# A hand-ordered attention stack: POOL's norm of attention a step later, squares and context for the unit four ahead

## What is computed

```python
x  = layernorm(x + mha(x, x, mask, bias))            # stage 0, LN of attention
x2 = layernorm(x + mha(x, ctx))                      # stage 1, LN of attention
x  = layernorm(x2 + gelu(x2 @ w1 + b1) @ w2 + b2)    # stage 1, feed-forward and its LN
q, c = rmsnorm(x, g_q), rmsnorm(ctx, g_c)            # stage 2, norm of the inputs
out = rmsnorm(x + mha(q, c) , g_out)                 # stage 2, norm of attention
```

## Time and profile before

| | |
|---|---|
| median of 3 runs | 727.37 us (725.52 to 729.23) |
| profiled execution, its own time | 729.24 us |
| its span | 727.4 us, mean granted TensorE clock 0.94 |
| busy: PE, DVE, ScalarE, POOL | 600.9, 443.3, 430.1, 339.7 us |

### The profile page before, as it was taken

One profiled execution on the slowest core, in us unless ns is written; L12 is line 12 of the kernel. 1 busy time (PEld: TensorE's weight loads), 2 busy tenths in 40 slices (PEclk: granted clock), 3 DMA queues, 4 the chain that ended last, 5 costly groups with the idle time before them and its releaser, 6 DMA issues.

```text
span 727.4 us, 17247 instructions
## 1 busy us (share of the span) xinstructions
PE 600.9 (83%) x6804; PEld 311.8 (43%) x6804; DVE 443.3 (61%) x884; ACT 430.1 (59%) x658; POOL 339.7 (47%) x642
## 2 busy tenths in 40 slices
PE   3699988886799999989896959688696968998984
PEld 1346555544344444544443425243344434443442
DVE  5324444435878887877673747566375758887831
ACT  2034444442267778786684756658485858886683
POOL 5234666654443544446246282635345365463212
PEclk9999999998889999999998989989798989999997
DMA  6723333433606625335260322406051515435000
GB/s 192 181 62 97 99 94 95 106 110 61 146 30 125 133 57 106 97 73 109 38 123 27 89 37 69 79 24 125 24 112 46 109 46 110 125 63 118 2 9 16
DMA packets 85382, 61.18 MB, mean 84 GB/s; under 512 B 5474, under 2 KB 84882, under 8 KB 85266
## 3 DMA queue, kind: packets, MB, share of 16 engines
q1 hardware_dynamic: 85176, 59.97, 36.2%
q10 hardware_dynamic: 126, 0.10, 0.0%
HBM read 33.25 MB, written 26.22 MB: 82 GB/s over the span
## 4 chain that ended last, share of the span: by engine, by line
PE 38%; POOL 19%; DMA 16%; DVE 9%; issue 8%; ACT 6%; SPq 4%; POOLq 0%; DVEq 0%; ACTq 0%
DMA kst<-k_parts 10%; PE pv L555 9%; PE dps L537 6%; DVE negmax L810 5%; DMA k_parts<-ks 4%; PE aps L505 4%; PE aps L608 3%; ACT probs L679 3%; PE dps L643 2%; POOL attn_z L967 2%; PE aps L587 2%; PE dps L626 2%; PE dps L530 2%; POOL ks L930 2%; PE dps L524 1%
## 5 line engine op out<-in xcount | busy, mean ns | idle before, releaser
L679 ACT ACTIVATE probs<-aps 128x1024 f32<-128x1024 f32 x288 | 293.7, 1024 | 206.0 <-PE aps L505 140.7
L810 DVE TENSOR_REDUCE negmax<-dps 128x1 f32<-128x512 f32 x512 | 324.1, 682 | 113.9 <-PE dps L537 112.7
L555 PE MATMUL pv<-probs,vp 128*32 128x256 f32 (+1 forms) x3072 | 162.8, 340 | 1.9 <-ACT raw L732 1.1
L537 PE MATMUL dps<-kst,qst 61*128 61x512 bf16 x512 | 130.0, 403 | 34.8 <-DMA kst<-k_parts 19.8
L505 PE MATMUL aps<-qst,kst 64*128 64x256 bf16 x1024 | 115.0, 278 | 5.6 <-ACT probs L679 5.4
L555 PEld LDWEIGHTS pv<-probs,vp 128*32 128x32 f32 x3072 | 71.7, 113 | 56.7 <-issue 23.5
L537 PEld LDWEIGHTS dps<-kst,qst 61*128 61x128 bf16 x512 | 32.2, 93 | 132.6 <-DVE negmax L810 74.3
L926 POOL TENSOR_TENSOR kr<-kf,ks 128x512 f32<-128x512 f32 (+1 forms) x24 | 23.9, 996 | 113.1 <-ACT ks L696 69.8
L837 DVE COPY mT<-dps 24x256 bf16<-24x256 bf16 x48 | 13.2, 274 | 91.3 <-PE dps L637 91.2
L505 PEld LDWEIGHTS aps<-qst,kst 64*128 64x128 bf16 x1024 | 48.9, 97 | 43.3 <-ACT probs L679 14.4
L806 DVE TENSOR_REDUCE negmax<-dps 128x4 f32<-128x512 f32 x64 | 42.9, 687 | 28.9 <-PE dps L530 28.9
(11 more groups left out here) (126 smaller groups left out, 841.4 us busy)
## 6 DMA issues: line engine op xcount, KB each, us to landing
kst<-k_parts SPq DMA_DIRECT2D x32, 384.0 KB, 6.8
qst<-q_parts SPq DMA_DIRECT2D x48, 192.0 KB, 3.8
k_parts<-ks SPq DMA_DIRECT2D x16, 384.0 KB, 2.6
q_parts<-qs SPq DMA_DIRECT2D x24, 192.0 KB, 1.9
cin<-in_ctx_dram SPq DMA_DIRECT2D x16, 256.0 KB, 5.3
k_parts<-ks SPq DMA_DIRECT2D x16, 256.0 KB, 3.0
q_parts<-qs SPq DMA_DIRECT2D x24, 128.0 KB, 1.9
k_parts<-ks SPq DMA_DIRECT2D x24, 128.0 KB, 3.0
```

The costliest lines, as they stand in the source:

```text
L537: mm = nc.tensor.matmul(dst, q[rows_in(g, 0, ROW_M), l, tile * P:(tile + 1) * P], k[rows_in(g, 0, ROW_M), l, :], start=True, stop=True)
L555: mm = nc.tensor.matmul(pv[32 * j:32 * j + 32, dst:dst + n], vp[u.parity][:, c, 4 * quad + j, :], probs[:, quad, src:src + n], start=(quad ...
L679: nc.scalar.activation(probs[:, quad, part * 1024:(part + 1) * 1024], src, ACT.Exp, scale=SCALE).then_inc(act_emptied, 1)
L810: ins = nc.vector.tensor_reduce(negmax[:, tile, at:at + 1], src, AX.X, ALU.max, negate=True)
```

## The change

Three things move, and no operation is added or removed.

1. POOL's `finish_attention` for a unit runs one step later: in step i for unit i-2 (`old`) in place of unit i-1. Within the step it stands right behind the split of K, ahead of `split_maxima(nxt, 0)`, where `main` is of stage 1 or 2, and right behind `split_maxima(nxt, 0)` where `main` is of stage 0. The last unit's is done after the loop.
2. ScalarE's squares are those of unit i+4 (`far`) in place of unit i+3, at the same places of the strings. POOL's `norm_inputs` still serves unit i+3.
3. SP loads the context of unit i+4 in place of i+3, behind the load of M1's rows in place of ahead of it, and stores a result one step later.

```diff
--- before.py
+++ after.py
@@ -86,10 +86,12 @@
 
 
 
+
     def __init__(self, i):
         self.i = i
         self.main, self.nxt, self.n, self.ahead = unit(i), unit(i + 1), unit(i + 2), unit(i + 3)
-        self.before = unit(i - 1)
+        self.far = unit(i + 4)
+        self.before, self.old = unit(i - 1), unit(i - 2)
         self.ffn, self.ffn_old = (u if u is not None and u.stage == 1 else None for u in (unit(i - 2), unit(i - 3)))
         self.items = [item for item in self.all_items() if item[1] is not None]
 
@@ -128,8 +130,8 @@
             elif name == "raw":
                 yield "raw", self.before, None
             elif name in SQUARES_OF:
-                ahead = self.ahead
-                yield "squares", ahead if ahead is not None and ahead.stage == 2 else None, SQUARES_OF[name]
+                far = self.far
+                yield "squares", far if far is not None and far.stage == 2 else None, SQUARES_OF[name]
             elif name == "B3":
                 known = self.before is not None
                 yield "values", self.before, (3, ALL if known and self.before.stage == 0 else (2, 3))
@@ -419,6 +421,11 @@
                     sp.dma_start(k[rows_in(g, 0, ROW_X), :, col:col + nk],
                                  kd_rows[:, LOCAL * g:LOCAL * g + LOCAL, 0:nk]).then_inc(stacks_loaded, 16)
 
+            def store_out(u):
+                sp.wait_ge(attn_norm.scaled, u.index + 1)
+                sp.dma_start(out[u.batch].rearrange("(t p) d -> p t d", p=P), attn_norm.zg[:, :, :]
+                             ).then_inc(out_stored, 16)
+
             def load_maxima(u, half):
                 mine = slice(LOCAL // 2 * half, LOCAL // 2 * half + LOCAL // 2)
                 sp.wait_ge(dve_emptied, DVE_AT[f"M{half}", u.index] + 1)
@@ -436,10 +443,10 @@
                 if s.i == 2:
                     sp.wait_ge(mask_made, 1)
                     sp.dma_start(kmd, kmask[:, :]).then_inc(mask_stored, 16)
-                if s.ahead is not None and s.ahead.stage > 0:
-                    load_context(s.ahead)
                 if s.main is not None:
                     load_maxima(s.main, 1)
+                if s.far is not None and s.far.stage > 0:
+                    load_context(s.far)
                 if s.n is not None:
                     if s.n.index == 2 * B:
                         sp.wait_ge(mask_stored, 16)
@@ -454,10 +461,9 @@
                     load_maxima(s.nxt, 0)
                 if s.n is not None and not early:
                     load_stacks(s.n)
-                if s.before is not None and s.before.stage == 2:
-                    sp.wait_ge(attn_norm.scaled, s.before.index + 1)
-                    sp.dma_start(out[s.before.batch].rearrange("(t p) d -> p t d", p=P), attn_norm.zg[:, :, :]
-                                 ).then_inc(out_stored, 16)
+                if s.old is not None and s.old.stage == 2:
+                    store_out(s.old)
+            store_out(unit(UNITS - 1))
             sp.wait_ge(out_stored, 16 * B)
 
         @block.tensor
@@ -1004,14 +1010,19 @@
                 if s.n is not None:
                     split(s.n, qf, qr, qs, LQ, "Q", q_steps)
                     split(s.n, kf, kr, ks, KEYS[s.n.stage], "K", k_steps)
+
+                late = s.main is not None and s.main.stage == 0
+                if s.old is not None and not late:
+                    finish_attention(s.old)
                 if s.nxt is not None:
                     split_maxima(s.nxt, 0)
+                if s.old is not None and late:
+                    finish_attention(s.old)
                 if s.ahead is not None and s.ahead.stage == 2:
                     norm_inputs(s.ahead)
                 if s.ffn_old is not None:
                     layer_norm(ffn_norm, s.ffn_old, in_cross(s.ffn_old), 2, xs[:, s.ffn_old.batch, :, :], x_ready)
-                if s.before is not None:
-                    finish_attention(s.before)
+            finish_attention(unit(UNITS - 1))
 
 
 # ---- launch: one core; constants of the shapes, and the weights laid out
```

## The result

The changed kernel takes 753.11 us (median of 4 runs, 749.47 to 757.41), against 728.3 of the kernel before in the same runs: a ratio of 1.0341, with a 95% interval of 1.0265 to 1.0417. It is 3.4% slower, where I had forecast 2.7% faster. The profiled execution took 749.47 us, its span is 747.7, the mean granted clock 0.926.

What follows compares the result with a forecast made beforehand. No engine bounds throughout; PE's waits at M1 for POOL's splits cost most, with the `kst` reload loop close behind. -35.2 -7.4 -5.2 +25.1 +3 = -19.7 us gives 707.7 from the 727.37 median; 8-in-10 range 692 to 722.

Steps and rivals of the forecast that it cites:

- (f): Context load, stores and ScalarE's six squares: zero effect, with 0.5 us in 12 steps on either side.
- (d): DVE's O waits for the norm, making M0 late in steps 8 to 21: 37.5 us, net cost 25.1.
- (e): New PE pauses of 1 to 2 us at O in cross-attention steps lower the clock: 3 us cost.
- signs of being wrong: PE waits over 2 us at M1, steps 14-19; steps 8-10 stay at 27 us; clock of steps 8-21 under 0.9.
- signs of being right: Among others: PE's `msplit` wait under 12 us, H 2.0 us, step 14 about 35 us, step 9 about 29.5.
- (a): M1's wait for POOL in steps 14 to 19 goes, as squares are ready a step early: gain 35.2 us.
- C: Rival: lower clock after each pause at O and again behind M0, 3.0 us in 14 steps: 746.7 us, chance 0.07.
- (b): The slow clock behind M1's wait, seen at H, goes in steps 14 to 19: gain 7.4 us.
- (c): M1's wait in self-attention steps 2 to 6, behind the norm of attention, goes: gain 5.2 us.
- Rival A: Wait at O costs next to nothing, reload of `kst` stays the bound: gain 47.8 us, 679.6 us, chance 0.08.
- the third that I gave it: Clock cost per pause at O in cross-attention steps, taken as a third of 1.5 us or of 9 in six steps: 3.

Runs made afterwards that it cites:

- the last run: Kernel before with squares for unit i+4 and two buffers of sums, context of unit i+4 moved ahead of the load of M1's rows: 677.71 us, ratio 0.9294.

## Why the prediction was wrong

**The step that failed is (f).** It put the squares at nothing: "ScalarE does the same six squares at the same places". I costed the operations and their places and did not follow their waits. That the squares must wait until POOL has read the sums of the unit before, now in the same step, is a wait of 50.0 us in 7 steps and 41.3 us of time, as the run with two buffers of sums shows. Its length comes of both moves together: where the norm does not stand between the keys' split and `nrs`, the same single buffer costs 17.9 or 18.1 us of wait and 16.0 or 15.3 us of time.

With that one term taken away, the total of my sum stands near the chip: -19.7 us was forecast, and 729.47 to 711.84, -17.6, was measured. That this is so close is in part luck, for its parts miss in both directions. In the profiled executions, against the kernel before:

| steps | my terms | two buffers of sums |
|---|---|---|
| up to M1 of step 7 | -5.2 | -8.4 |
| 7 to 12 | +10.6 | +18.9 |
| 12 to 19 | -32.9 | -35.7 |
| 19 to 22 | +7.8 | +8.1 |

(My terms per stretch are the -35.2, -7.4 and -5.2, the delays of M0 in (d) less 0.9 of cover in each of steps 8 to 21, and 0.5 of (e) in each of steps 8 to 10 and 19 to 21.) The cost in steps 8 to 11 was put too small by some 8 us, and the rest came out better by about 6.

None of my signs of being wrong showed in the changed kernel: M1 of steps 14 to 19 waits for nothing, steps 8 to 10 take 30.6 to 31.1 us, and the granted clock from M1 of step 8 to that of step 21 is 0.93. Of the signs of being right, step 14 failed most clearly, with 41.0 us where I had named about 35. I had named no sign for a wait of ScalarE.

(a) itself said that the squares "are ready a step early": true for POOL, at ScalarE's cost. C, to which I gave a chance of 0.07 for the slower side, names another mechanism: with two buffers of sums the pauses at O are still there and the kernel is faster than the one before, so the clock behind them did not make the change slow. That C's 746.7 lies near 753.11 is luck.

**(a) M1's wait in steps 14 to 19** is gone, 0 in place of 35.2 us. Right. But in the changed kernel it was given back at V of the step before.

**(b) H's slow clock** went with the wait, 1.99 us in place of 3.54. Right for H; in the changed kernel the lower clock came behind the new wait, V taking 2.08 us.

**(c) Self-attention.** The five steps from M1 of step 1 to that of step 6 take 16.83 us (17.03 the last) in place of 17.9, 5.3 us together. Right.

**(d) and (e) O's wait.** The lengths were right: 3.27 us in step 9 (3.3 to 3.4 forecast) and 2.80 in step 15 (2.8 for a feed-forward step). What follows was too small in steps 8 to 11: M0 moved 4.9 us against its keys' split in step 9, not 3.4, and steps 8 to 10 of the run with two buffers are 4.1 to 5.4 us longer than before, where (d) and (e) gave 3 (3.4 less 0.9 of cover, and 0.5). Step 11, already with feed-forward, is 4.8 longer where 1.5 was forecast. (d) also counted the pairs of maxima between O and M0 one too low: the strings have three in a cross-attention step and two in a feed-forward one, of which PE gets one pair through before the ring holds it.

The term that shows itself too small is (e). In step 9 PE waits 2.09 and 1.03 us behind O and V takes 2.07 us, where V took 1.16 before. It is so in steps 8, 9 and 10 of the changed kernel (2.08, 2.07, 2.07), and with two buffers of sums in 8 and 9, and in part in 10 (2.07, 2.08, 1.70). In step 8 PE is busy 26.35 us for its 262 matmuls at a granted clock of 0.94; before, step 9 had the same number in 24.79 at 1.00. How much of the 4.1 to 5.4 us is pace and how much is wait, no run tells apart. The durations of V's matmuls over several steps follow (ns minimum/median/maximum; first the changed kernel, then before). The first line mixes several cases: beside steps 8 to 10 it holds steps 13 and 14 with the pause for the squares, step 6, and step 7, whose V ran at the lower pace before too:

```profile
L602 PE MATMUL aps<-win,xc x72: 274/421/582, 155.2 to 426.4; 128*128 128x128 f32 x72
```

```profile
L596 PE MATMUL aps<-win,xc x64: 275/275/580, 193.7 to 414.2; 128*128 128x128 f32 x64
```

The feed-forward steps from 12 on were sized better: 33.9 to 34.3 us in steps 12 to 16 with two buffers, about 35 forecast. There V comes before PE has to wait, and keeps its 1.16 us.

**The Trainium skill's rule** ("TensorE: Matmul & The Clock Gate", section "A second HAM failure mode: psum-queue depth-cycling") agrees with the rows of steps 8 to 10 better than the third that I gave it: with pauses such as the 2.09 and 1.03 us at PSUM entries in step 9, V ran at the lower pace. As an explanation of the whole loss it would be wrong: the kernel with the same waits at O and two buffers of sums is 2.5% faster than the kernel before.

**Rival A,** that the wait at O costs nothing, was refuted where I had put it. Its number, 679.6, is near what the kernel before reaches with early squares and two buffers (675.9), where the norm does not hold O.

## What to carry to other kernels

When work is moved a step earlier, look at both ends of its buffers: the wait for its inputs goes, and the wait for the reader of what it overwrites comes, in a line that the diff does not show. A list of every wait of the moved instruction, with the step in which its counter is now raised, would have shown the wait of ScalarE; one more buffer of 6 columns took it away. And in-order queues have places that are free and places that are not: with two buffers of sums, steps 8 to 10 and 19 to 21 take 3.7 to 5.5 us more with the norm behind the keys' split than with the norm in the idle time ahead of Q's split, six instructions earlier.

## What the hardware showed unexpectedly

From M1 of step 0 to M1 of step 1, where all kernels here issue the same matmuls, the ten profiled executions take between 15.75 and 19.33 us. The stretches, of the kernel before and of the changed one:

```profile
40.70:60.03 19.33, 19.16 (x292) 10.60 (x291) 6.34 (x11) 6.21 (x12) 6.84 (x17) 1.00 0.33 85
```

```profile
39.48:55.23 15.75, 14.38 (x291) 8.49 (x290) 6.27 (x11) 6.21 (x12) 6.85 (x17) 1.00 0.42 104
```

PE is busy 19.16 us in the one and 14.38 in the other with the same matmuls, DVE, ScalarE and POOL alike in both, and the granted clock reads 1.00 in both. The kernel before with early squares took 18.39 with one buffer of sums and 15.78 with two. The times follow none of the changes, so I take this for a matter of the execution, though no kernel was profiled twice to show it; then 3.6 of the 11.4 us that the changed kernel is ahead at step 7 are no effect of the change. The granted clock of a stretch did not show the slower pace here; the duration of PE's instructions did.

The context's load, 5.3 us to landing, takes 2.8 us in the changed kernel, 4.0 with the norm alone moved, and 3.3 in the last run, where it stands ahead of M1's rows again but is that of unit i+4. Why it is shorter is not shown, and its place in the queue moved the time of the kernel by nothing that the last run could show.
